# Softmax inverse sums: PE transposes against a VectorE transpose with a round trip through DRAM, and the normalization at another tile

## The chip, the cores and the metric

The kernel runs on one core of a Trainium2 chip. The metric is the device time of one execution in microseconds (us), the median of several. The core's engines run in parallel, each through its own list of instructions in order, and wait for one another through semaphores: TensorE (PE, matmuls; PEld its weight loads), VectorE (DVE), ScalarE (ACT), GpSimd (POOL), and SyncE (SP), which here issues every DMA. The sixteen DMA engines of the core work off what SP issues.

## The reference

Two layers, each added to its input. The first is an attention over 512 tokens with 16 heads of 32, modulated by a conditioning vector; the second rotates quaternions (its filter is the same for all frequencies, so it is a product with a constant matrix). Shapes: x is (8, 512, 512). Cut to what matters:

```python
q, k, v = (proj(Wq), proj(Wk), proj(Wv))                    # H = 16, D = 32
scores = jnp.einsum('bhsd,bhtd->bhst', q, k) * scale
scores = jnp.where(mask[None, None, :, :], -jnp.inf, scores)
attn = jax.nn.softmax(scores, axis=-1)
out = jnp.einsum('bhst,bhtd->bhsd', attn, v)                # -> (B, S, E)
out = out @ Wo.T
rms = jnp.sqrt(jnp.mean(out * out, axis=-1, keepdims=True) + EPS)
xn = out / rms * rms_scale
xn = xn * (1.0 + sc[:, None, :]) + shift[:, None, :]        # sc, shift from the conditioning
x = x + xn
x = x + rotated(x)                                          # Hamilton products with constants
```

The softmax is not normalized in place: the kernel multiplies exp(scores) with v first and scales the result by the inverse of the row sums afterwards.

## The kernel before

**Stages.** `projections` computes q, k and v of all eight batches and leaves them in DRAM (`q_scratch`, `k_scratch`, `v_scratch`). `attention` follows; the change is in it alone.

**Units and tiles.** Attention works in U = 32 units, one for each batch b and group g of four heads (u = 4 b + g). A unit has 16 tiles, one for each head i and block c of 128 query tokens; tile n = 16 u + t is 128 x 512. A tile passes through: `score` on PE (9 tiles ahead), `mask` on DVE (adds the mask, takes the row minimum, into `probs`; some 6 ahead), `exp` on ACT (2 ahead; the row sums go to `den`), `turn` on PE (four 128x128 transposes into one half of `turn_ps`), `move_out` (into `turned_probs`, by DVE for even tiles, ACT for odd). When all 16 tiles of unit u are out, `values(u)` on PE multiplies them with v, at t = 1 of unit u + 1, into `value_ps`: 128 partitions (four heads of 32 dims) by 512 tokens.

**The inverse sums before.** `den` holds a sum per query token on the partitions (128 x 16), but `value_ps` has query tokens along its free axis. So the inverse has to be turned and repeated over the 32 dims of each head: `invert` on DVE at t = 0 (L698), `spread_inverse` on POOL copies it out to 128 x 4 x 128 (L869), `turn_scale` on PE at t = 1, behind `values`, turns that with four transposes into a half of `turn_ps` (L624), `move_scale` on ACT copies it to `inv_T` (L824). `place` counts the halves of `turn_ps`, since the scale takes a 17th place in each unit.

**The norm and what follows.** `norm(u)` on DVE (L713) at t = 3 writes `o_T` = `value_ps` times `inv_T`. POOL's `split` waits for it and cuts o_T into `o_hi` and `o_lo` (L878, L880); POOL then does, in the same iteration and in this order, `rotate` (L518, L911, L913) and `shift` (L888) for a chunk of 128 tokens of the batch before. `project` on PE multiplies o_hi and o_lo with Wo for that batch, one product a tile from t = 2 to 13; `square` (ACT), `rms` (POOL), `rescale` and `residual` (DVE) finish a chunk in the next unit.

**SP's order.** In iteration u SP does: `load_x` for chunk u - 4 (L559), which waits for the rotation of chunk u - 6; `store` of the rotated chunk u - 6 (L563), which waits for the same; `load_unit(u + 2)`, 2 MB of q and k in eight DMAs (L57, L59), which waits until all tiles of unit u are scored (PE gets there at t = 6); where g = 0 `load_mod`, where g = 1 `load_v`. The rotation of chunk u - 6 stands in POOL's iteration u - 1. SP issues in this order and stops at each wait.

**What sets the order.** It is written out by hand: constants (`NORM_AT`, `INVERT_AT`, ...) give the tile at which a step stands, `MASKS` and `EXPS` how many masks and exps DVE and ACT do at each.

Of the kernel before, what the change touches and what calls it, by code (L numbers as in the profile page):

```python
# [8 lines left out]
F32 = mybir.dt.float32  # L9
# [4 lines left out]
P = 128  # L14
# [12 lines left out]
VALUES_AT, SCALE_AT, PROJECT_AT = (1,), 1, 2  # L27
NORM_AT, INVERT_AT, RESCALE_AT, RESIDUAL_AT, SQUARE_AT = 3, 0, 1, 2, 0
# [392 lines left out]
def attention(nc, x, scr, rows, late, qk_stored, mod_scr, out, mask_bias, rot, ident, wo_hi, wo_lo):  # L421
# [3 lines left out]
    with ExitStack() as ctx:  # L425
# [14 lines left out]
        inv = sb("inv", [P, HG, TC])  # L440
        inv_d = sb("inv_d", [P, TC, HG, D])
# [29 lines left out]
        inverted, spread = sem("inverted"), sem("spread")  # L471
        scale_turned, scale_out = sem("scale_turned"), sem("scale_out")
# [14 lines left out]
        def place(n):  # L487

            return n + (n + TILES - SCALE_AT) // TILES - 1

        def scale_place(u):

            return place(min(TILES * (u + 1) + SCALE_AT, N) - 1) + 1

        AT = {place(n): n for n in range(N)}

# [4 lines left out]
        def place_free(eng, at):  # L501

            if at == SCALE_AT - 1:
                at -= 2
            if at in AT and by_act(AT[at]):
                eng.wait_ge(out_act, AT[at] // 2 + 1)
            elif at in AT:
                eng.wait_ge(out_dve, AT[at] // 2 + 1)
            elif at >= SCALE_AT:
                eng.wait_ge(scale_out, (at + 1) // (TILES + 1))  # L510
# [29 lines left out]
        def _(sp):  # L540
# [9 lines left out]

            def load_mod(b):
                if b >= 2:
                    sp.wait_ge(summed, TC * (b - 1))
                sp.dma_start(mod[:, b % 2], mod_scr[b].partition_broadcast(P)).then_inc(mod_in[b % 2], 16)
# [13 lines left out]
            for u in range(U):  # L568
# [29 lines left out]
        def _(pe):  # L598
# [11 lines left out]
            def turn(n):  # L610

                pe.wait_ge(exped, n + 1)
                place_free(pe, place(n) - 2)
                for j in range(TC):
                    last = pe.transpose(turn_ps[:, place(n) % 2, j * P:(j + 1) * P], probs[:, n % RING, j * P:(j + 1) * P],  # L615
                                        ident[:, :])
# [390 lines left out]
```

## Time and profile before

| | us |
|---|---|
| median of 3 runs (lowest, highest) | 912.03 (911.07, 912.26) |
| the profiled execution, its own time | 911.68 |
| its span in the profile | 909.9 |
| PE busy in the span | 854.2 |
| DVE, ACT, POOL busy | 641.4, 613.3, 488.1 |

The attention stage begins near 283 us, and its first inverse is at 303 us; the last tile is turned at about 866 us. Behind that is a tail of some 40 us for the last chunks. The profile lists, for each engine, when it is busy and what ended the idle time before an instruction; "landing" of a DMA is the time from its issue to its semaphore.

### The profile page before, as it was taken

The numbers are of one execution on the slowest core, as the hardware profiler recorded it, in microseconds if no ns is written. First come the engines' busy times: TensorE is split into PE (matmuls) and PEld (weight loads), VectorE is DVE, ScalarE is ACT, GpSimd is POOL, SyncE is SP. The second block draws the span as 40 slices with busy tenths as digits, with TensorE's granted clock in tenths as the row PEclk, the third lists the DMA queues.
The fourth block names the chain that finished last, engine by engine and source line by source line (L and its number), as shares of the span: only waits on it lengthen the run. The fifth ranks groups of instructions, "written<-read, shape, count | busy, mean of one in ns | idle before, by whom it ended". The sixth has DMA issues, their size and how long they took to land.

```text
span 909.9 us, 16967 instructions
## 1 busy us (share of the span) xinstructions
PE 854.2 (94%) x5254; PEld 633.0 (70%) x5254; DVE 641.4 (70%) x1514; ACT 613.3 (67%) x1491; POOL 488.1 (54%) x348
## 2 busy tenths in 40 slices
PE   6999999999995999999999999999999999999970
PEld 5788888888883655776677667766776677667740
DVE  4621321322216887999899989998999899989868
ACT  5222232322215989899989998999899989998920
POOL 0999980000000111377577757775777577757774
PEclk9999999999997999999999999999999999999995
DMA  8844654553497784587667775777578568765201
GB/s 279 327 165 177 226 195 164 217 196 143 181 197 244 167 181 105 140 204 161 159 173 159 162 201 128 161 180 184 128 180 207 137 146 209 159 160 117 70 24 46
DMA packets 82305, 153.74 MB, mean 169 GB/s; under 512 B 8472, under 2 KB 9112, under 8 KB 82224
## 3 DMA queue, kind: packets, MB, share of 16 engines
q1 hardware_dynamic: 82224, 152.75, 62.4%
q8 instruction: 39, 0.64, 0.3%
q14 instruction: 42, 0.34, 0.1%
HBM read 102.35 MB, written 50.36 MB: 168 GB/s over the span
## 4 chain that ended last, share of the span: by engine, by line
PE 58%; DVE 7%; issue 3%; DVEq 0%; ACT 0%; POOL 0%; ACTq 0%
PE turn_ps L615 23%; PE value_ps L641 13%; PE score_ps L607 12%; PE y_ps L657 8%; DVE probs L690 3%; PE turn_ps L624 2%; DVE turned_probs L705 1%; PE score_ps L657 1%; DVE probs L518 1%; DVE probs L764 0%; DVE v_sb L776 0%; DVE least L690 0%; DVE o_T L713 0%; DVEq L514 0%; DVE probs L767 0%
## 5 line engine op out<-in xcount | busy, mean ns | idle before, releaser
L807 ACT ACTIVATE probs<-probs,least 128x512 f32<-128x512 f32 x512 | 363.5, 713 | 4.2 <-DVE least L690 4.1
L690 DVE CUSTOM_DVE_ANT_0 probs<-score_ps,mask_bias 128x512 f32<-128x512 f32 x512 | 331.5, 681 | 38.7 <-PE score_ps L607 36.0
L615 PE MATMUL turn_ps<-ident,probs 128*128 128x128 f32 x2048 | 309.3, 273 | 9.9 <-DVE turned_probs L705 3.9
L615 PEld LDWEIGHTS turn_ps<-ident,probs 128*128 128x128 f32 x2048 | 245.4, 141 | 86.3 <-issue 30.2
L607 PE MATMUL score_ps<-k_rows,q_rows 128*128 128x512 f32 x512 | 247.3, 485 | 9.7 <-PEq L68 9.4
L705 DVE COPY turned_probs<-turn_ps 128x512 f32<-128x512 f32 x256 | 175.9, 687 | 16.2 <-PE turn_ps L615 16.2
L816 ACT ACTIVATE turned_probs<-turn_ps 128x512 f32<-128x512 f32 x256 | 150.9, 590 | 51.2 <-PE turn_ps L615 50.5
L261 DVE SCALAR_TENSOR_TENSOR late<-proj,late 128x512 fp32r<-128x512 f32 x64 | 43.9, 690 | 182.2 <-ACT late L230 182.2
L230 ACT ACTIVATE late<-proj 128x512 fp32r<-128x512 f32 x64 | 38.3, 598 | 128.2 <-PE proj L319 113.2
L518 POOL TENSOR_TENSOR late<-rot,late 128x2048 f32<-128x2048 f32 x27 | 124.3, 4605 | 0.0
L641 PE MATMUL value_ps<-turned_probs,v_sb 128*32 128x512 f32 x1024 | 116.5, 595 | 0.7 <-ACT turned_probs L816 0.7
L878 POOL CAST o_hi<-o_T 128x512 fp32r<-128x512 f32 x32 | 21.4, 670 | 165.4 <-DVE o_T L713 134.5
L607 PEld LDWEIGHTS score_ps<-k_rows,q_rows 128*128 128x128 f32 x512 | 97.8, 191 | 14.0 <-issue 9.8
L807 ACT ACTIVATION_READ_ACCUMULATOR probs<-probs,least 128x1 f32 x512 | 97.7, 191 | 0.0
L915 POOL MEMSET minus_half<- 128x1 f32 x1 | 0.1, 98 | 150.4 <-POOLq L68 150.4
L641 PEld LDWEIGHTS value_ps<-turned_probs,v_sb 128*32 128x32 f32 x1024 | 30.0, 109 | 63.6 <-issue 62.6
L911 POOL TENSOR_TENSOR late<-late 128x1024 f32<-128x1024 f32 x27 | 64.6, 2392 | 2.1
L222 ACT ACTIVATE v_out<-proj 128x512 f32<-128x512 f32 x32 | 18.9, 597 | 62.8 <-PE proj L319 62.8
L317 PE MATMUL proj<-w_hi_v,x_hi 128*128 128x512 f32 x128 | 51.5, 402 | 7.2 <-DVE x_lo L270 7.2
L318 PE MATMUL proj<-w_lo_v,x_hi 128*128 128x512 f32 x128 | 50.9, 398 | 0.0
L319 PE MATMUL proj<-w_hi_v,x_lo 128*128 128x512 f32 x128 | 50.8, 397 | 0.0
L869 POOL COPY inv_d<-inv 128x512 f32<-128x512 f32 x32 | 19.6, 613 | 56.4 <-DVE inv L698 56.4
(112 smaller groups left out, 1289.3 us busy)
## 6 DMA issues: line engine op xcount, KB each, us to landing
q_rows<-q_scratch SPq DMA_DIRECT2D x128, 256.0 KB, 6.0
k_rows<-k_scratch SPq DMA_DIRECT2D x128, 256.0 KB, 6.9
q_scratch<-late SPq DMA_DIRECT2D x64, 256.0 KB, 2.3
k_scratch<-late SPq DMA_DIRECT2D x64, 256.0 KB, 2.3
v_scratch<-v_out SPq DMA_DIRECT2D x32, 256.0 KB, 2.0
v_sb<-v_scratch SPq DMA_DIRECT2D x8, 1024.0 KB, 12.0
raw<-in_xT SPq DMA_DIRECT2D x7, 1024.0 KB, 5.7
late<-in_x SPq DMA_DIRECT2D x28, 256.0 KB, 6.0
```

The costliest lines, as they stand in the source:

```text
L317: pe.matmul(out, hi(k), other_hi(k), start=(k == 0), stop=False)
L318: pe.matmul(out, hi(k), other_lo(k), start=False, stop=False)
L518: return eng.tensor_tensor(to.rearrange("p j (i d) -> p j i d", i=4), rot[:, :, :, :], chunk.rearrange("p (j d) -> p j d", j=4).unsqueeze( ...
L607: pe.matmul(score_ps[:, n % 4, :], rows.q[:, u % 2, i, c * P:(c + 1) * P], rows.k[:, u % 2, i, :], start=True, stop=True).then_inc(scored, 1)
L615: last = pe.transpose(turn_ps[:, place(n) % 2, j * P:(j + 1) * P], probs[:, n % RING, j * P:(j + 1) * P], ident[:, :])
L641: last = pe.matmul(value_ps[i * D:(i + 1) * D, :], v_sb[:, b % 2, j, h * D:(h + 1) * D], turned_probs[:, (HG * u + i) % SLOTS, j, :], star ...
L657: last = pe.matmul(y, left[:, b % 2, k, t], right[:, k, :], start=(part == 0), stop=(part == 11))
L690: dve.tensor_tensor_reduce(probs[:, n % RING, :], score_ps[:, n % 4, :], mask_bias[:, c, :], 1.0, 3e38, ALU.add, ALU.min, least[:, n // TI ...
L705: dve.tensor_copy(turned_probs[:, h % SLOTS, :, n % TC * P:(n % TC + 1) * P], turn_ps[:, place(n) % 2, :].rearrange("p (j t) -> p j t", j= ...
L807: act.activation(probs[:, n % RING, :], probs[:, n % RING, :], ACT.Exp, bias=least[:, u % 2, n % TILES:n % TILES + 1], scale=-1.0, accum_o ...
L816: act.activation(turned_probs[:, h % SLOTS, :, n % TC * P:(n % TC + 1) * P], turn_ps[:, place(n) % 2, :].rearrange("p (j t) -> p j t", j=T ...
L911: pool.tensor_tensor(mix[:, 0:2, :], mix[:, 0:2, :], mix[:, 2:4, :], ALU.add).then_inc(paired, 1)
```

## The change

The inverse no longer passes through POOL, PE and ACT. DVE writes the reciprocals into the first 16 columns of a 128 x 32 tile (the rest is set to zero once), and turns that by its transpose of 32 x 32 blocks into `inv_turn`: each of the four blocks of 32 partitions then has the 16 sums as rows and 32 query tokens as columns. SP writes the four blocks into a DRAM tensor of 16 x 128 (`inv_scratch`), waits until they have landed, and reads from it for each of the four heads one row of 512 elements into 32 partitions of `inv_T`. The norm waits for these four loads, and stands at t = 6 instead of 3. `turn_scale`, `move_scale`, POOL's `spread_inverse` and the 17th place of `turn_ps` are gone; tile n now uses half n % 2, and its `turn` waits for the copy of tile n - 2.

```diff
-VALUES_AT, SCALE_AT, PROJECT_AT = (1,), 1, 2
-NORM_AT, INVERT_AT, RESCALE_AT, RESIDUAL_AT, SQUARE_AT = 3, 0, 1, 2, 0
+VALUES_AT, PROJECT_AT = (1,), 2
+NORM_AT, INVERT_AT, RESCALE_AT, RESIDUAL_AT, SQUARE_AT = 6, 0, 1, 2, 0
...
-        inv = sb("inv", [P, HG, TC])
-        inv_d = sb("inv_d", [P, TC, HG, D])
+        inv = sb("inv", [P, 32])
+        inv_turn = sb("inv_turn", [P, 32])
...
+        def moved_out(eng, n):
+
+            if n >= 0:
+                eng.wait_ge(out_act if by_act(n) else out_dve, n // 2 + 1)
...
+            def spread_inverse(u):
+                sp.wait_ge(inv_turned, u + 1)
+                if u > 0:
+                    for i in range(HG):
+                        sp.wait_ge(inv_in[i], 16 * u)
+                for a in range(TC):
+                    sp.dma_start(scr["inv"][:, a * D:(a + 1) * D],
+                                 inv_turn[a * D:a * D + TILES, :]).then_inc(inv_stored, 16)
+                sp.wait_ge(inv_stored, 64 * (u + 1))
+                if u > 0:
+                    sp.wait_ge(normed, u)
+                for i in range(HG):
+                    sp.dma_start(inv_T[i * D:(i + 1) * D, :],
+                                 scr["inv"][i * TC:(i + 1) * TC, :].rearrange("c q -> (c q)").partition_broadcast(D)
+                                 ).then_inc(inv_in[i], 16)
...
                 if u >= NG + 2:
                     store((u - NG - 2) // NG, (u - NG - 2) % NG)
+                if u > 0:
+                    spread_inverse(u - 1)
                 if u + 2 < U:
                     load_unit(u + 2)
...
+            spread_inverse(U - 1)
             sp.wait_ge(valued, NG * (B - 1))
...
                 pe.wait_ge(exped, n + 1)
-                place_free(pe, place(n) - 2)
+                moved_out(pe, n - 2)
...
-            def turn_scale(u):
-
-                pe.wait_ge(spread, u + 1)
-                place_free(pe, scale_place(u) - 2)
-                for c in range(TC):
-                    last = pe.transpose(turn_ps[:, scale_place(u) % 2, c * P:(c + 1) * P],
-                                        inv_d[:, c].rearrange("p i d -> p (i d)"), ident[:, :])
-                last.then_inc(scale_turned, 1)
...
                 if u > 0:
-                    dve.wait_ge(spread, u)
-                dve.reciprocal(inv[:, :, :], den[:, u % 2]).then_inc(inverted, 1)
+                    dve.wait_ge(inv_turned, u)
+                dve.reciprocal(inv[:, 0:TILES].rearrange("p (i c) -> p i c", i=HG), den[:, u % 2]).then_inc(inverted, 1)
+                dve.wait_ge(inverted, u + 1)
+                if u > 0:
+                    dve.wait_ge(inv_stored, 64 * u)
+                dve.transpose(inv_turn[:, :], inv[:, :]).then_inc(inv_turned, 1)
...
                 dve.wait_ge(valued, u + 1)
-                dve.wait_ge(scale_out, u + 1)
+                for i in range(HG):
+                    dve.wait_ge(inv_in[i], 16 * (u + 1))
...
-            def move_scale(u):
-                act.wait_ge(scale_turned, u + 1)
-                if u > 0:
-                    act.wait_ge(normed, u)
-                act.activation(inv_T[:, :], turn_ps[:, scale_place(u) % 2, :], ACT.Copy).then_inc(scale_out, 1)
...
-            def spread_inverse(u):
-                pool.wait_ge(inverted, u + 1)
-                if u > 0:
-                    pool.wait_ge(scale_turned, u)
-                pool.tensor_copy(inv_d[:, :, :, :], inv[:, :, :].rearrange("p i c -> p c i").unsqueeze(3)
-                                 .to_broadcast([P, TC, HG, D])).then_inc(spread, 1)
...
+    scr["inv"] = nc.dram_tensor("inv_scratch", (TILES, P), F32, kind="Internal").ap()
```

SP's list in the middle of attention, at the end of an iteration with g = 0 and the start of the next, before (`late<-in_x` is load_x, `out<-late` the store):

```order
L554 DMA mod_b<-mod_scratch 128x1024 [waits summed]
L559 DMA late<-in_x 128x512 [waits rotated]
L563 DMA out<-late 128x512 [waits rotated]
L57 DMA q_rows<-q_scratch 32x4x512 [waits scored]
L59 DMA k_rows<-k_scratch 32x4x512
```

and after:

```order
L555 DMA mod_b<-mod_scratch 128x1024 [waits summed]
L560 DMA late<-in_x 128x512 [waits rotated]
L564 DMA out<-late 128x512 [waits rotated]
L542 DMA inv_scratch<-inv_turn 16x32 [waits inv_in2,inv_in1,inv_in3,inv_in0,inv_turned]
L542 DMA inv_scratch<-inv_turn 16x32 x3
L548 DMA inv_T<-inv_scratch 32x512 [waits normed,inv_stored]
L548 DMA inv_T<-inv_scratch 32x512 x3
L57 DMA q_rows<-q_scratch 32x4x512 [waits scored]
```

The eight DMAs of the inverse, with two waits, now stand between the store and the loads of q and k.

DVE's list around the old place of the norm (t = 2 and 3 of a unit), before; the rows L690 are the masks, L705 the copies of turned tiles, L729 the residual:

```order
L729 SCALAR_TENSOR_TENSOR late<-scaled,rstd,late 128x512 [waits shifted,rstd_ready,scaled_ready]
L690 ISA probs,least<-score_ps,mask_bias 128x512 [waits scored,turned]
L690 ISA least 128x1
L713 TENSOR_TENSOR o_T<-value_ps,inv_T 128x512 [waits o_ready,scale_out,valued]
L705 COPY turned_probs<-turn_ps 128x4x128 [waits valued,turned]
```

and from there to its new place (t = 5 to 7), after, where the masks are L682 and the copies L701:

```order
L701 COPY turned_probs<-turn_ps 128x4x128 [waits valued,turned]
L682 ISA probs,least<-score_ps,mask_bias 128x512 [waits scored,turned]
L682 ISA least 128x1
L710 TENSOR_TENSOR o_T<-value_ps,inv_T 128x512 [waits inv_in2,inv_in3,inv_in1,o_ready,inv_in0,valued]
L682 ISA probs,least<-score_ps,mask_bias 128x512 [waits scored,turned]
L682 ISA least 128x1
L701 COPY turned_probs<-turn_ps 128x4x128 [waits valued,turned]
```

The norm has moved from ahead of the copy of tile 2 to ahead of a mask and the copy of tile 6, and waits for the four loads instead of ACT's copy.

## Rows read from the trace of the kernel before

**Rows 1.** Page, parts 1 and 4: busy us (share) xinstructions; chain by engine.

```profile
PE 854.2 (94%) x5254; PEld 633.0 (70%) x5254; DVE 641.4 (70%) x1514; ACT 613.3 (67%) x1491; POOL 488.1 (54%) x348
...
PE 58%; DVE 7%; issue 3%; DVEq 0%; ACT 0%; POOL 0%; ACTq 0%
```

**Rows 2.** Windows: busy us of PE, PEld, DVE, ACT, POOL (instructions), clock, DMA, GB/s.

```profile
400.00:500.00 100.00, 99.32 (x701) 72.43 (x700) 92.28 (x244) 91.22 (x237) 72.10 (x49) 1.00 0.69 160
```

**Rows 3.** Timeline, DVE: start, duration, line, tiles; norms (L713) and reciprocals (L698).

```profile
381.46 0.69 DVE L713 TENSOR_TENSOR o_T<-value_ps,inv_T 128x512 f32<-128x512 f32 x1
...
575.34 0.24 DVE L698 RECIPROCAL inv<-den 128x16 f32<-128x16 f32 x1
...
581.42 0.69 DVE L713 TENSOR_TENSOR o_T<-value_ps,inv_T 128x512 f32<-128x512 f32 x1
...
854.59 0.69 DVE L713 TENSOR_TENSOR o_T<-value_ps,inv_T 128x512 f32<-128x512 f32 x1
...
865.59 0.24 DVE L698 RECIPROCAL inv<-den 128x16 f32<-128x16 f32 x1
871.22 0.69 DVE L713 TENSOR_TENSOR o_T<-value_ps,inv_T 128x512 f32<-128x512 f32 x1 [1.89 <-ACT inv_T L824]
```

**Rows 4.** Chain in order of time: start, us; the four transposes of one unit.

```profile
852.93 0.59 PE turn_ps L624 x4
```

**Rows 5.** Timeline, DVE and PE, around the copy of tile 6.

```profile
585.09 0.68 DVE L690 CUSTOM_DVE_ANT_0 probs<-score_ps,mask_bias 128x512 f32<-128x512 f32 x1
...
585.70 0.68 DVE L705 COPY turned_probs<-turn_ps 128x512 f32<-128x512 f32 x1
...
586.86 0.60 PE L615 MATMUL turn_ps<-ident,probs 128*128 128x128 f32 x4
```

**Rows 6.** SP's waits (us in total, times, longest); timeline of POOL, subtraction and rotation.

```profile
SPq L559 <- POOL late L913: 108.8, 26, 17.4
...
582.97 1.30 POOL L880 TENSOR_TENSOR o_lo<-o_T,o_hi 128x512 fp32r<-128x512 f32 x1
...
591.37 1.29 POOL L913 TENSOR_TENSOR late<-late 128x512 f32<-128x512 f32 x1
```

**Rows 7.** Timeline, SP: start of each DMA issue, its us, line, tiles.

```profile
585.01 0.33 SPq L57 DMA_DIRECT2D q_rows<-q_scratch  x1
...
592.68 0.35 SPq L559 DMA_DIRECT2D late<-in_x  x1
593.07 0.44 SPq L563 DMA_DIRECT2D out<-late  x1
603.22 0.33 SPq L57 DMA_DIRECT2D q_rows<-q_scratch  x1
603.59 0.43 SPq L59 DMA_DIRECT2D k_rows<-k_scratch  x1
604.07 0.43 SPq L57 DMA_DIRECT2D q_rows<-q_scratch  x1
...
611.25 0.90 SPq L563 DMA_DIRECT2D out<-late  x1
```

**Rows 8.** DMA us to landing, issued 865.81, 847.64, 593.07, 611.25; then two busy windows.

```profile
out<-late SPq DMA_DIRECT2D x1, 256.0 KB, 2.0
...
late<-in_x SPq DMA_DIRECT2D x1, 256.0 KB, 2.7
...
out<-late SPq DMA_DIRECT2D x1, 256.0 KB, 7.4
...
out<-late SPq DMA_DIRECT2D x1, 256.0 KB, 9.4
...
588.00:590.00 2.00, 2.00 (x17) 1.73 (x15) 2.00 (x7) 2.00 (x6) 1.92 (x2) 1.00 1.05 205
...
616.00:618.00 2.00, 2.00 (x17) 1.51 (x14) 1.02 (x4) 2.00 (x6) 0.00 (x0) 1.00 1.04 383
```

**Rows 9.** Chain in order of time: PE's last products.

```profile
870.50 9.11 PE score_ps L657 x39
```

More of the change, by code:

```diff
@@ L470, in attention @@
         out_act, out_dve = sem("out_act"), sem("out_dve")
-        inverted, spread = sem("inverted"), sem("spread")
-        scale_turned, scale_out = sem("scale_turned"), sem("scale_out")
+        inv_set, inverted, inv_turned = sem("inv_set"), sem("inverted"), sem("inv_turned")
+        inv_stored = sem("inv_stored")
+        inv_in = [sem(f"inv_in{i}") for i in range(HG)]
         valued, normed = sem("valued"), sem("normed")
@@ L485, in attention @@
         rotated = sem("rotated")
[L487 to L495, printed above, removed]
         def by_act(n):
             return n % 2 == 1
[L501 to L510, printed above, removed]
+        def moved_out(eng, n):
+            if n >= 0:
+                eng.wait_ge(out_act if by_act(n) else out_dve, n // 2 + 1)
         def take_waits(eng):
@@ L612, in turn @@
                 pe.wait_ge(exped, n + 1)
-                place_free(pe, place(n) - 2)
+                moved_out(pe, n - 2)
                 for j in range(TC):
-                    last = pe.transpose(turn_ps[:, place(n) % 2, j * P:(j + 1) * P], probs[:, n % RING, j * P:(j + 1) * P],
+                    last = pe.transpose(turn_ps[:, n % 2, j * P:(j + 1) * P], probs[:, n % RING, j * P:(j + 1) * P],
                                         ident[:, :])
                 last.then_inc(turned, 1)
-            def turn_scale(u):
-                pe.wait_ge(spread, u + 1)
-                place_free(pe, scale_place(u) - 2)
-                for c in range(TC):
-                    last = pe.transpose(turn_ps[:, scale_place(u) % 2, c * P:(c + 1) * P],
-                                        inv_d[:, c].rearrange("p i d -> p (i d)"), ident[:, :])
-                last.then_inc(scale_turned, 1)
             def values(u, part):
@@ L666, in _ @@
                     values(u - 1, VALUES_AT.index(t))
-                if t == SCALE_AT and u > 0:
-                    turn_scale(u - 1)
                 if n + SCORE_AHEAD < N:
@@ L675, in _ @@
                 values(U - 1, part)
-            turn_scale(U - 1)
             for parts in (range(9), range(9, 12)):
@@ L705, in move_out @@
                 dve.tensor_copy(turned_probs[:, h % SLOTS, :, n % TC * P:(n % TC + 1) * P],
-                                turn_ps[:, place(n) % 2, :].rearrange("p (j t) -> p j t", j=TC)).then_inc(out_dve, 1)
+                                turn_ps[:, n % 2, :].rearrange("p (j t) -> p j t", j=TC)).then_inc(out_dve, 1)
             def norm(u):
                 dve.wait_ge(valued, u + 1)
-                dve.wait_ge(scale_out, u + 1)
+                for i in range(HG):
+                    dve.wait_ge(inv_in[i], 16 * (u + 1))
                 if u > 0:
@@ L730, in residual @@
                                          ALU.mult, ALU.add).then_inc(summed, 1)
-            done = 0
+            dve.memset(inv[:, :], 0.0).then_inc(inv_set, 1)
+            dve.wait_ge(inv_set, 1)
             for n in range(MASK_AHEAD):
@@ L816, in move_out @@
                 act.activation(turned_probs[:, h % SLOTS, :, n % TC * P:(n % TC + 1) * P],
-                               turn_ps[:, place(n) % 2, :].rearrange("p (j t) -> p j t", j=TC),
+                               turn_ps[:, n % 2, :].rearrange("p (j t) -> p j t", j=TC),
                                ACT.Copy).then_inc(out_act, 1)
-            def move_scale(u):
-                act.wait_ge(scale_turned, u + 1)
-                if u > 0:
-                    act.wait_ge(normed, u)
-                act.activation(inv_T[:, :], turn_ps[:, scale_place(u) % 2, :], ACT.Copy).then_inc(scale_out, 1)
             def square(m):
@@ L846, in _ @@
                     square(u - NG - 1)
-                if t == SCALE_AT and u > 0:
-                    move_scale(u - 1)
                 if by_act(n - 1) and n > 0:
@@ L852, in _ @@
             square(CHUNKS - 1)
-            move_scale(U - 1)
             for c in range(TC):
@@ L917, in _ @@
             for u in range(U):
-                if u > 0:
-                    spread_inverse(u - 1)
                 if u > NG:
@@ L927, in _ @@
                     shift(u - NG)
-            spread_inverse(U - 1)
             rms(CHUNKS - 1)
```

## The prediction

> **What bounds the kernel now.** I read first the page's busy shares and chain, then the busy time by windows, because the share over the whole span mixes the projection stage with the attention stage that the change edits. TensorE is busy 94% of the span, and of the chain that ended last 58% is PE [rows 1]. In the attention stage it is plainer: from 400 to 500 us PE is busy 99.3 of 100 us, while DVE and ACT stand at 92 and 91 [rows 2]. So a microsecond of PE work is worth a microsecond there, and DVE and ACT have about 8% to spare. The repeating piece is a unit (16 tiles). From the norm (L713) of unit 5 to that of unit 31 there are 26 intervals: 854.59 - 381.46 = 473.1 us, or **18.20 us a unit** [rows 3]. An edit that touches every unit is judged against this number.
>
> **What is removed.** Each of the 32 units loses four PE transposes (L624), the ACT copy (L824) and the POOL copy (L869). The four transposes take 0.59 us of the chain [rows 4], and as PE is the bound they are worth that: the floor of a unit falls to 18.20 - 0.59 = **17.6 us**. ACT's and POOL's part lies off the path and is worth nothing by itself. The slot that the scale took in the two-deep turn_ps ring goes too; I give it nothing, since PE hardly waits.
>
> **What is added on DVE.** One 32x32 transpose of 128x32, with a wait for the reciprocal before it. The trace has no such transpose; the nearest rows are the reciprocal of 128x16 (0.24 us) [rows 3] and a 128x512 copy (0.68 us) [rows 5], so it costs 0.1 to 0.7 us a unit, and I take 0.3, near the small one. DVE has some 1.4 us a unit free (8% of 18.2), so the path sees nothing of it; the masks queued behind it have no late customer either, because PE is then in the value matmuls. If that cover were gone, 0.3 us a unit would come on top, 10 us in all. The memset ahead of the loop is one instruction, in a stretch where DVE waits for scores.
>
> **What is moved: the norm, and what hangs on it.** The norm goes from t=3 to t=6. Behind it on DVE are a mask and the copy of tile 6, and PE's turn of tile 8 waits for that copy. In the unit shown that turn starts at 586.86, and the copy takes 0.68 us [rows 5]; with norm and mask ahead of it at 0.61 us each (585.70 less 585.09, the pitch at which DVE starts such operations), the norm must start by 586.86 - 0.68 - 0.61 - 0.61, about 584.9. That is 3.5 us after its old place (581.42), 9.5 us after the reciprocal (575.34) [rows 3], and 8.9 us after it once PE's 0.59 us are gone. Taken from the reciprocal alone, the new route fits. That is not where it starts, though.
>
> **The queue that the route is put into.** SP runs in order, and the eight new DMAs are written behind load_x and store of the same iteration. Both wait for POOL's rotation of the iteration before; SP waits there 26 times, 108.8 us in all [rows 6]. That rotation stands on POOL behind split, which waits for the norm. So the norm of one unit now gates the inverse of the next unit, and that gates the next norm: **a loop once round per unit that did not exist before**. If it is longer than 17.6 us, its length sets the time.
>
> Step by step. From the norm's start (581.42 [rows 3]) through POOL's cast, subtraction and rotation, whose last step ends at 591.37 + 1.29 = 592.66 [rows 6], to SP's load_x at 592.68 [rows 7] it is **11.26 us**. The POOL copy that is removed stood ahead of split's wait, so nothing of this shrinks. From load_x to store 0.39 us, and DMAs behind one another start every 0.47 us (603.59, 604.07) [rows 7]: the first store of the inverse starts 0.86 us after load_x, the fourth 1.41 later. It lands after L1; the next four start over another 1.41 us, and the last lands after L2. With 0.05 us for SP to wake, a loop is 11.26 + 0.86 + 1.41 + L1 + 0.05 + 1.41 + L2 = **15.0 + L1 + L2**.
>
> L1 and L2 are not in the trace: stores of 16x32 elements, and loads of 64 KB that read one row for 32 partitions. The nearest rows are 256 KB transfers on an empty queue: a store lands in 2.0 us, a load in 2.7 [rows 8]. These are the upper ends. For the lower ends I take the moving of 256 KB out of them, 0.7 us at 383 GB/s for the store and 1.3 us at 205 for the load, the fast and the slow rate at which busy windows run [rows 8]; that leaves 1.3 and 1.4. I choose 1.8 and 2.2, nearer the upper ends, because four transfers of small pieces have no reason to land at the very floor. Then a loop is **19.0 us**, 1.4 over the floor (bounds 17.7 and 19.7).
>
> The Trainium skill (DMA: Bandwidth & Descriptors, section "Anatomy of one DMA — SWDGE (gpsimd) path") gives a DMA about 2.0 us of fixed cost, mostly the receipt of the write and heaviest at HBM, plus its bytes at 436 GB/s. That speaks against two hops through DRAM; by it L1 would be an estimated 2.0 and L2 2.15, the loop 19.15, and the sum some 3 us higher. For a 256 KB store it would give 2.6 us where the row shows 2.0, so the trace's own rows are used.
>
> **Queueing.** All of it shares one queue. From the first q load of a unit to the landing of its store, a unit with the modulation load takes 593.07 + 7.4 - 585.01 = 15.5 us, one with the v load 611.25 + 9.4 - 603.22 = 17.4 [rows 7, 8]; a plain unit is shorter. In the loop the q loads come 1 to 1.6 us before the norm (behind the inverse loads, when PE has scored the sixth tile while DVE still waits), and the 256 KB of inverse loads, 1.2 us, are added. So the store lands 15.5 + 1.2 - 1 = 15.7 or 17.4 + 1.2 - 1.6 = 17.0 us after the norm, and the inverse stores 0.2 behind it. By themselves they would land at 11.26 + 0.86 + 1.41 + 1.8 = 15.3. So the modulation unit is held up by 0.6, the v unit by 1.9, the plain one not: loops of 19.0, 19.6 and 20.9 us. Of the 26 loops 14 are plain and 6 each of the others: (14 x 19.0 + 6 x 19.6 + 6 x 20.9) / 26 = **19.6 us**, 1.4 over the 18.20 of now, or 26 x 1.4 = +36 us.
>
> **Before and behind the loops.** Units 1 to 5 have no rotation in the loop; each gains its 0.59 us, as does the tail: 6 x 0.59 = -3.5 us. In the tail the inverse lands 0.5 + 1.41 + 1.8 + 0.05 + 1.41 + 2.2 = 7.4 us after the last reciprocal (865.59), at 873.0 where the norm now is at 871.22 [rows 3]. PE first runs 36 of its 48 last products, which need nothing of it: until about 870.50 - 0.59 + 36/48 x 9.11 = 876.7 [rows 9]. From a norm's start to the end of the subtraction it is 582.97 + 1.30 - 581.42 = 2.9 us [rows 3, 6], so that ends at 875.9 and just fits. If that cover is gone, at most the 1.8 us of delay are lost.
>
> **Sum.** 909.9 + 36 - 3.5 = 942 us of span; the profiled execution took 911.68, 1.8 more than its span, and the median is 0.35 above it: **944 us**, 3.5% slower.
>
> **The rivals.**
> (a) *The loop does not bind, and the kernel is faster.* One mechanism: both hops land so fast that the loop stays under 17.6 us, that is L1 + L2 under 2.6 us with no queueing. Then each of 32 units keeps its 0.59 us: 912 - 19 = 893. For it: SP's wait and POOL's idle time are harmless today, and from the reciprocal alone there would be 8.9 us. Against it: the lower ends that I could find sum to 2.7, and the modulation and v units still queue. 8%.
> (b) *About the same* (910 to 914): L1 + L2 near 3.2 and hardly any queueing. 4%.
> (c) *The queue decides in every unit*: small writes, or reads of one row, land late, or the 2 MB of q and k hold up all units as I have it for the v units. All loops of 21 us: 909.9 + 26 x 2.8 - 3.5 + 2.2 = 981. 13%.
> (d) The forecast: slower by the loop, 918 to 972 us. 75%. With L1 + L2 at 2.7 the plain loops would be near 18.1, but the queue would end last in the others (15.5 + 1.2 + 0.2 + 2.9 = 19.8, and 20.1): 19.0 on average and 929 us. With 2.0 and 2.7, 19.7 plain and 20.1 on average, 957 us; 0.5 us more on each hop gives another 15 to 26 us.
>
> The range of 915 to 975 leaves out (a), (b) and most of (c). Changes below 0.2% (1.8 us) can hardly be told from none; faster by more has 8%, within it 4%, slower 88%.
>
> **What would show it.** Right: the norm's interval from unit 6 on is 18.5 to 21 us instead of 18.20, with a period of four units; DVE idles 1 to 3 us ahead of the norm, released by a load of inv_T; PE waits ahead of the turn of tile 8; SP's first inverse store starts 0.9 us after load_x, not after the transpose; from norm to load_x it is still 11.26 us. The first units should be shorter than now. Wrong: SP waiting at the inverse store for DVE's transpose rather than at load_x for POOL, no idle time ahead of the norm, or two hops that together land in under 2.7 us.

## The result and the profile after

Line numbers of the changed kernel: reciprocal L690, DVE's transpose L694, norm L710, residual L726; SP's stores of the inverse L542, its loads L548, load_x L560, store L564; PE's turn L619, score L611, tail products L652; POOL's split L860 and L862, rotation L503, L893, L895, rms L881.

| | before | after |
|---|---|---|
| median us (lowest to highest) | 911.81 (4 runs) | 952.01 (949.39 to 953.22, 4 runs) |
| ratio | | 1.0438 (1.0414 to 1.0462) |
| span of the profiled execution | 909.9 | 947.5 |
| norm of iteration 5 to that of iteration 31 | 473.1 | 508.27 |
| a unit (26 of them) | 18.20 | 19.55 |

The profiled execution of the changed kernel took 949.39 us, the shortest of its four. One of the four runs of e8 below, 947.24 us, was in a slow state of the chip; the ratio there leaves it out, the median does not.

The page of the changed kernel, busy time and the chain by engine, against [rows 1]:

```profile
PE 846.5 (89%) x5126; PEld 620.1 (65%) x5126; DVE 655.6 (69%) x1547; ACT 602.8 (64%) x1459; POOL 468.7 (49%) x316
...
POOL 28%; DMA 10%; issue 10%; SPq 9%; DVE 7%; PE 5%; DVEq 0%; POOLq 0%
```

PE's share of the chain that ended last fell from 58% to 5%; POOL, the DMAs and SP's queue took its place. The stretch of [rows 2] again:

```profile
400.00:500.00 100.00, 88.39 (x619) 61.71 (x618) 85.63 (x226) 81.39 (x211) 60.50 (x40) 1.00 0.69 162
```

PE is no longer full: 88.4 of 100 us instead of 99.3. One plain unit, DVE's timeline of the changed kernel:

```profile
583.17 0.69 DVE L710 TENSOR_TENSOR o_T<-value_ps,inv_T 128x512 f32<-128x512 f32 x1
...
591.96 0.24 DVE L690 RECIPROCAL inv<-den 128x16 f32<-128x16 f32 x1
592.23 0.21 DVE L694 STREAM_TRANSPOSE inv_turn<-inv 128x32 f32<-128x32 f32 x1
...
602.18 0.69 DVE L710 TENSOR_TENSOR o_T<-value_ps,inv_T 128x512 f32<-128x512 f32 x1 [0.88 <-DMA inv_T<-inv_scratch]
```

and SP's timeline in the same unit:

```profile
594.43 0.35 SPq L560 DMA_DIRECT2D late<-in_x  x1
594.83 0.62 SPq L564 DMA_DIRECT2D out<-late  x1
595.62 1.76 SPq L542 DMA_DIRECT2D inv_scratch<-inv_turn  x4
598.56 1.70 SPq L548 DMA_DIRECT2D inv_T<-inv_scratch  x4
```

The turned inverse is ready at 592.44, but SP's first store of it starts at 595.62, behind load_x at 594.43, which is 11.26 us after the norm of 583.17. That is the loop: 11.26 to load_x, 1.19 to the first store, 2.94 to the first load, 3.62 to the next norm, 19.01 in all. The waits of the whole span, first DVE's and PE's, then SP's:

```profile
PE turn_ps L619 <- DVE turned_probs L701: 44.8, 36, 2.9
...
DVE o_T L710 <- DMA inv_T<-inv_scratch: 37.6, 27, 2.6
```

```profile
SPq L560 <- POOL late L895: 224.8, 26, 13.0
...
SPq L548 <- DMA inv_scratch<-inv_turn: 55.0, 32, 3.8
```

SP's wait at load_x doubled against [rows 6] (224.8 instead of 108.8 us). It is now a wait with customers: the norm stands 27 times for the inverse, and PE's turns stand behind it.

### The profile page after: what moved, and what is told of

Read it like the earlier page. It is cut to its first block, busy times and chain, and to the rows that moved or that the text cites. A ratio compares the mean times of both kernels' runs of the same rounds, so it can differ in the third digit from the quotient of the medians.

```text
span 947.5 us, 17028 instructions
## 1 busy us (share of the span) xinstructions
PE 846.5 (89%) x5126; PEld 620.1 (65%) x5126; DVE 655.6 (69%) x1547; ACT 602.8 (64%) x1459; POOL 468.7 (49%) x316
## 4 chain that ended last, share of the span: by engine, by line
POOL 28%; DMA 10%; issue 10%; SPq 9%; DVE 7%; PE 5%; DVEq 0%; POOLq 0%
POOL late L503 12%; POOL late L893 6%; DMA inv_scratch<-inv_turn 5%; DMA inv_T<-inv_scratch 5%; SPq L542 4%; POOL o_lo L862 4%; POOL late L895 3%; SPq L548 3%; DVE probs L682 2%; PE turn_ps L619 2%; POOL o_hi L860 2%; DVE o_T L710 2%; PE value_ps L636 2%; SPq L564 1%; DVE turned_probs L701 1%
## 5 line engine op out<-in xcount | busy, mean ns | idle before, releaser
L619 PE MATMUL turn_ps<-ident,probs 128*128 128x128 f32 x2048 | 312.4, 275 | 53.5 <-DVE turned_probs L701 44.8
L682 DVE CUSTOM_DVE_ANT_0 probs<-score_ps,mask_bias 128x512 f32<-128x512 f32 x512 | 335.4, 684 | 7.5 <-PE score_ps L611 7.5
L619 PEld LDWEIGHTS turn_ps<-ident,probs 128*128 128x128 f32 x2048 | 243.0, 141 | 134.6 <-issue 54.9
L611 PE MATMUL score_ps<-k_rows,q_rows 128*128 128x512 f32 x512 | 247.2, 486 | 9.2 <-PEq L68 9.1
L701 DVE COPY turned_probs<-turn_ps 128x512 f32<-128x512 f32 x256 | 176.0, 687 | 19.2 <-PE turn_ps L619 19.1
L860 POOL CAST o_hi<-o_T 128x512 fp32r<-128x512 f32 x32 | 21.4, 669 | 275.7 <-DVE o_T L710 234.3
L611 PEld LDWEIGHTS score_ps<-k_rows,q_rows 128*128 128x128 f32 x512 | 98.5, 193 | 39.8 <-DVE least L682 28.1
L503 POOL TENSOR_TENSOR late<-rot,late 128x2048 f32<-128x2048 f32 x27 | 124.2, 4601 | 0.0
L893 POOL TENSOR_TENSOR late<-late 128x1024 f32<-128x1024 f32 x27 | 64.1, 2375 | 2.1
L222 ACT ACTIVATE v_out<-proj 128x512 f32<-128x512 f32 x32 | 18.9, 597 | 62.6 <-PE proj L319 62.6
L317 PE MATMUL proj<-x_hi,w_hi_k 128*128 128x512 f32 x128 | 49.8, 389 | 0.0
```

What stands on the lines that cost most here:

```text
L317: pe.matmul(out, hi(k), other_hi(k), start=(k == 0), stop=False)
L503: return eng.tensor_tensor(to.rearrange("p j (i d) -> p j i d", i=4), rot[:, :, :, :], chunk.rearrange("p (j d) -> p j d", j=4).unsqueeze( ...
L611: pe.matmul(score_ps[:, n % 4, :], rows.q[:, u % 2, i, c * P:(c + 1) * P], rows.k[:, u % 2, i, :], start=True, stop=True).then_inc(scored, 1)
L619: last = pe.transpose(turn_ps[:, n % 2, j * P:(j + 1) * P], probs[:, n % RING, j * P:(j + 1) * P], ident[:, :])
L682: dve.tensor_tensor_reduce(probs[:, n % RING, :], score_ps[:, n % 4, :], mask_bias[:, c, :], 1.0, 3e38, ALU.add, ALU.min, least[:, n // TI ...
L701: dve.tensor_copy(turned_probs[:, h % SLOTS, :, n % TC * P:(n % TC + 1) * P], turn_ps[:, n % 2, :].rearrange("p (j t) -> p j t", j=TC)).th ...
```

## The experiments

All medians are of 4 runs; the kernel before took 911.1 to 911.9 us beside them. "A unit" is the mean over the 26 intervals of the norm from iteration 5 to 31, "plain" the usual interval with no held-up inverse; both are of the profiled execution, which can lie some us beside the median (934.09 against 939.03 us in e1).

| kernel | us | ratio to before | a unit | plain |
|---|---|---|---|---|
| e1_inverse_first | 939.03 | 1.0315 (1.0285 to 1.0344) | 18.95 | 18.05 |
| e2_norm_at_8 | 965.21 | 1.0596 (1.0579 to 1.0614) | 20.17 | 20.2 |
| e4_short_rotation | 940.58 | 1.0302 (1.0263 to 1.0341) | 19.16 | 18.05 |
| e5_before_norm_6 | 923.30 | 1.0135 (1.0118 to 1.0152) | 18.53 | 18.53 |
| e7_loads_early | 944.35 | 1.0334 (1.0292 to 1.0376) | 19.47 | 18.05 |
| e8_shift_first | 936.35 | 1.0230 (1.0210 to 1.0251) | 19.24 | 18.05 |
| e9_residual_4 | 949.87 | 1.0401 (1.0357 to 1.0446) | 19.50 | 18.71 |
| e10_shift_only | 951.32 | 1.0434 (1.0416 to 1.0451) | 19.53 | 19.0 |
| e11_v_on_act | 919.79 | 1.0093 (1.0076 to 1.0110) | 18.34 | 18.05 |
| e12_values_split | 928.01 | 1.0187 (1.0169 to 1.0204) | 18.69 | 18.38 |
| e14_before_split | 918.07 | 1.0069 (1.0052 to 1.0086) | 18.46 | 18.46 |
| e15_norm_at_3 | 894.42 | 0.9810 (0.9794 to 0.9826) | 17.67 | 17.67 |

My theory was the loop through load_x. Against it stood explanations in which POOL's rotation has no part: the inverse's own way from the reciprocal to the norm, or the queue of q, k and v.

**The loop through load_x, cut.** Only SP's list changes:

```diff
+                if u > 0:
+                    spread_inverse(u - 1)
                 if u >= NG:
                     load_x(b - 1, g)
                 if u >= NG + 2:
                     store((u - NG - 2) // NG, (u - NG - 2) % NG)
-                if u > 0:
-                    spread_inverse(u - 1)
```

> One edit to the changed kernel: SP issues the eight DMAs of the inverse ahead of load_x and store in each iteration, so that they no longer stand behind POOL's rotation; nothing else. Theory A (the loop norm, split, rotation, load_x, inverse, norm sets 19.55 us a unit): the loop is cut. The inverse then starts 0.5 us after the reciprocal; in plain units it lands some 7 us after it where 8.9 are allowed, so the unit falls to the floor of PE near 17.6; units with the modulation or the v load ahead in the queue stall by some 0.6 and 2.8 us. Average about 18.4, span 915 to 922, ratio to before 1.00 to 1.01. SP's wait at load_x for POOL disappears or shrinks to under 30 us in all. Theory B (the round trip through DRAM is too long for tile 6 wherever it starts): 940 to 952, ratio 1.03 to 1.045. Theory C (contention of the DMAs with q and k): no great change either, above 940.

13 us came back, less than expected: 939 us lies just under what theories B and C had, so the median doesn't decide between them and A. The single units do. SP's waits of e1 no longer list load_x; it waits for DVE's transpose instead:

```profile
SPq L542 <- DVE inv_turn L694: 187.6, 32, 10.1
...
SPq L548 <- DMA inv_scratch<-inv_turn: 87.4, 32, 6.6
```

Plain units fell from 19.01 to 18.05, with no wait at the norm: the loop was real, and worth 0.96 a unit. But 18.05 is not my floor of 17.6, and something else took up to 3 us in some units. The next runs are about both.

**The same loop, shortened on POOL.** The middle addition of the rotation works on 64 columns instead of 1024:

```diff
-                pool.tensor_tensor(mix[:, 0:2, :], mix[:, 0:2, :], mix[:, 2:4, :], ALU.add).then_inc(paired, 1)
+                pool.tensor_tensor(mix[:, 0:1, 0:64], mix[:, 0:1, 0:64], mix[:, 2:3, 0:64], ALU.add).then_inc(paired, 1)
```

> Left out: of POOL's middle addition in the rotation of a chunk (128x1024, 2.4 us) all but 64 columns, so the rotated chunks of the main part are not the reference's; all waits stay. The loop becomes some 2.2 us shorter from norm to load_x (11.26 to about 9.1 us). Theory A: the unit falls by 0.7 to 1.9 us, to 17.7 to 18.8 (the queue behind q and k, or PE's floor, then ends last), so 900 to 930, though POOL is idle for more than 6 us of each unit in the changed kernel. Theories B and C (length of the round trip alone, contention of DMAs): POOL is half idle and off the path, no change, 945 to 955.

The addition fell from 2.37 to 0.32 us and the kernel by 11 us, although POOL is busy for half of the span only. The time, 940.58 us, is outside theory A's 900 to 930 and outside the 945 to 955 of B and C. What it shows is that the length of POOL's rotation counts: explanations without POOL in the path fall. The shortest units again end at 18.05, so 17.0 for the loop (19.0 - 2.05) was not reached: the same second bound.

**The norm later still.**

```diff
-NORM_AT, INVERT_AT, RESCALE_AT, RESIDUAL_AT, SQUARE_AT = 6, 0, 1, 2, 0
+NORM_AT, INVERT_AT, RESCALE_AT, RESIDUAL_AT, SQUARE_AT = 8, 0, 1, 2, 0
```

> One number in the changed kernel: the norm stands at tile 8 instead of 6, 1.8 us later on PE. Theory A (loop): the deadline moves, but so does the start, since load_x follows the norm by a fixed 11.26 us; the unit stays at 19.5 us, ratio to before 1.035 to 1.05. Theory B (the round trip is measured from the reciprocal and misses tile 6 by 1.0 to 2.3 us): the stalls of plain units go to zero and those of v units to 0.5, 26 x 1.3 = 34 us less, about 915, ratio 1.00 to 1.01.

Slower than either expectation. The norm never waits for a DMA; DVE waits for POOL (e2, timeline of DVE):

```profile
588.64 0.68 DVE L710 TENSOR_TENSOR o_T<-value_ps,inv_T 128x512 f32<-128x512 f32 x1
...
602.08 0.75 DVE L726 SCALAR_TENSOR_TENSOR late<-scaled,rstd,late 128x512 f32<-128x512 f32 x1 [2.90 <-POOL rstd L881]
...
608.82 0.69 DVE L710 TENSOR_TENSOR o_T<-value_ps,inv_T 128x512 f32<-128x512 f32 x1
```

A second loop: norm, split, rotation, shift, rms on POOL, residual on DVE 13.44 us later, and 6.74 us to the next norm, 20.18. At t = 6 the same sum is 13.49 + 4.55 = 18.04 in e1 (norm 441.23, residual 454.72, norm 459.27). That fits the 18.05 so well that I took it for the second bound (theory L2). It was wrong, as the next runs show.

**The norm's place alone.** The kernel before with `NORM_AT` 6 instead of 3, everything else as it was.

> The kernel before with one number changed: the norm at tile 6 instead of 3, the inverse still through POOL, PE and ACT. Theory A: the norm's place alone costs nothing, since nothing there closes the loop (the inverse does not wait for POOL's rotation through SP): 910 to 914, ratio 0.998 to 1.003, with SP's wait at load_x some 2.7 us longer in each unit. A rival by which the later norm itself costs the time (POOL's work, the products of the batch before, or the next unit's residual come late): up to 26 x 1.35 = 35 us more, 930 to 950.

12 us slower, where I had expected nothing. The first units have no rotation, no rescale and no residual yet, and they are as long as the others (e5, DVE's timeline):

```profile
330.98 0.68 DVE L713 TENSOR_TENSOR o_T<-value_ps,inv_T 128x512 f32<-128x512 f32 x1
...
349.49 0.69 DVE L713 TENSOR_TENSOR o_T<-value_ps,inv_T 128x512 f32<-128x512 f32 x1
```

18.51, where the kernel before has 17.93 there: 0.58, nearly the 0.61 at which DVE starts such operations. It speaks for a theory without POOL (D): at t = 3 DVE stands anyway, because PE is in the value products and delivers no scores; at t = 6 it has no free time, and the norm pushes the masks and copies on which PE's turns wait. PE's waits for DVE's copies in two of these units, in e5 (321.23 to 358.27) and then in the kernel before (320.95 to 356.81), bear it out:

```profile
PE turn_ps L615 <- DVE turned_probs L705: 2.9, 6, 0.9
```

```profile
PE turn_ps L615 <- DVE turned_probs L705: 1.7, 6, 0.3
```

That is 0.6 us more in each unit, the whole difference. In the later units the place costs less, 0.33 (18.53 against 18.20).

**L2 against D.** Three kernels share a base, e7, in which SP has the inverse first and the modulation and v loads ahead of `load_unit`. e8 adds `shift` ahead of `split` on POOL, e9 instead puts the residual at t = 4 (`RESIDUAL_AT` 4). e10 has e8's order on POOL, but SP's list of the changed kernel.

> The changed kernel with SyncE's list put in another order: the inverse's DMAs first in a unit (as in e1_inverse_first), and the modulation and v loads ahead of the next rows' load instead of behind it. Theory V (what e1 still lost behind a v load is the queue: the 1 MB is issued late in a unit, just ahead of the next unit's inverse, the norm then waits 1.7 to 3.0 us, TensorE stands over 2 us and runs at a lower granted clock afterwards): the waits behind v loads and the slow stretches after them go, all units take the 18.05 us of e1's plain ones; e1 had 18.95 on average over 26 intervals, so its span of 932.2 falls by about 23 to 909, some 911 us in all, ratio 1.00. Theory W (the low clock has another cause than the wait, or the load's bytes disturb whatever place they have): units behind a v load stay near 20, 930 us or more.

> e7_loads_early with GpSimd's list in another order as well: the addition of the shift to the next block of x ahead of the split of o instead of behind the rotation. Theory L2 (e1's 18.05 us of a unit are a second loop: norm, split, rotation, shift 1.3, rms and rstd on GpSimd, residual, norm): that loop gets 1.3 shorter, another bound ends it at 17.6 to 17.8, and 26 intervals give 6 to 11 us: 900 to 905 us, ratio 0.988 to 0.994. Theory D (the 18.05 are the round of VectorE and TensorE over one unit, in which the norm at the seventh tile stands among VectorE's work instead of in its wait for TensorE): shift's place does nothing, the same time as e7.

> e7_loads_early with VectorE's residual at the fifth tile of a unit instead of the third. Theory L2 (the second loop through GpSimd sets 18.05): the residual no longer waits for rstd, and the loop gets about 2 us of slack: units of 17.6 to 17.8, as in e8. Theory D (round of VectorE and TensorE): the residual leaves VectorE's wait for TensorE in the third tile and stands in a stretch where VectorE has no free time, so a unit gets longer by up to its 0.67 us: 18.4 to 18.7, 920 to 928 us, slower than e7.

> The changed kernel as it is, SyncE's list untouched, with GpSimd's shift ahead of the split alone. Theory L1 (in the changed kernel the loop norm, split, rotation, x load, store, inverse DMAs, norm binds at 19.0 in plain units; shift is not in it): the norm still waits for the inverse's DMA in nearly every unit, plain units stay at 19.0, 947 to 955 us. Theory L2 (the second loop binds here too): 1.0 to 1.3 less in a unit, 915 to 925 us.

L2 falls twice. With the shift out of its way (e8) plain units stay at 18.04; with two tiles of slack for the residual (e9) they get longer, 18.71. Timeline of DVE in e9:

```profile
598.51 0.75 DVE L726 SCALAR_TENSOR_TENSOR late<-scaled,rstd,late 128x512 f32<-128x512 f32 x1
601.00 0.69 DVE L710 TENSOR_TENSOR o_T<-value_ps,inv_T 128x512 f32<-128x512 f32 x1
...
619.70 0.69 DVE L710 TENSOR_TENSOR o_T<-value_ps,inv_T 128x512 f32<-128x512 f32 x1
```

The residual waits for nothing there, and costs 0.66 a unit merely by standing later on DVE, as D says. The medians are no test here, because the waits of e7 behind v loads (below) stay in e8 and e9 too: e9 took 949.87 us against D's 920 to 928, and e8's runs (931 to 947) overlap those of e7 (937 to 946). e10 confirms the loop through load_x in the changed kernel: shift is not in it, and nothing moved (19.0 plain, 951.32 against 952.01).

e7 itself missed. Its plain units are e1's, but behind five of the six v loads the norm waits 3.4 to 6.4 us (1.7 to 3.0 in e1). SP's timeline of e7 behind a v load, and the landing of these stores:

```profile
464.86 1.71 SPq L542 DMA_DIRECT2D inv_scratch<-inv_turn  x4
474.79 1.70 SPq L548 DMA_DIRECT2D inv_T<-inv_scratch  x4
```

```profile
inv_scratch<-inv_turn SPq DMA_DIRECT2D x4, 2.0 KB, 6.9
```

Four stores of 2 KB took 9.9 us from the first issue to the loads. x, out, v, q and k, 3.5 MB, had been issued on the same queue 5 to 12 us earlier, and I put it down to them. Another place in that queue doesn't help.

**The v load on ScalarE's queue.** e1, with the v load issued by ACT at t = 2 of the unit, ahead of SP's q and k loads (queue and place change together here; which of them did it isn't separated):

```diff
-                if g == 1 and b + 1 < B:
-                    load_v(b + 1)
...
+                if t == 2 and u % NG == 1 and u // NG + 1 < B:
+                    load_v(u // NG + 1)
```

> e1_inverse_first with the v load (1 MB once in four units) issued by ScalarE at the third tile of its unit, so on another DMA queue and in the stretch in which the queue of SyncE stands empty, instead of by SyncE behind the next rows' load. Theory Q (what e1, and more so e7, lost in the unit behind a v load: the inverse's four small stores stand in the same queue behind 3.5 MB instead of 2.5 MB, and the engines take some 200 GB/s while the rotation runs): the norm's waits behind v loads fall from 1.7 to 3.0 us to under 0.7, the low clock behind them goes too, all units come near 18.05, and of e1's 23 us of excess over 26 units some 18 to 23 go: a span of 909 to 914, 911 to 916 us, ratio 1.00 to 1.005. Theory W (1 MB more in the unit disturbs whatever queue and place it has): the waits stay over 1.5 us, 930 to 940 us.

Most of what Q says: 19 us less than e1, though 4 more than its range. No unit behind a v load waits any more; what is left is 1.2 to 1.7 us in the v unit itself, whose inverse loads now run beside it (iteration 29 has a modulation load ahead of it as they have, but no v load, and its norm doesn't wait):

```profile
461.86 0.69 DVE L708 TENSOR_TENSOR o_T<-value_ps,inv_T 128x512 f32<-128x512 f32 x1 [1.72 <-DMA inv_T<-inv_scratch]
```

**The value products in two pieces.** e11, and the kernel before, with `VALUES_AT = (1, 2)`.

> e11_v_on_act with the 32 value products of a unit put at two tiles in TensorE's list (16 at the second, 16 at the third) instead of all at the second. Theory D (the 18.05 us of e7, e8 and e11 are a round of VectorE and TensorE: VectorE stands still while TensorE runs 3.6 us of value products, and the norm at the seventh tile no longer fills that stand): with half the block each time VectorE stands less, and a unit comes to 17.5 to 17.8, 6 to 14 us less than e11: 900 to 908 us, ratio 0.987 to 0.997. Against it (the round is set by TensorE's own work): 18.05 as before, the time of e11.

> The kernel before with its value products at two tiles in the same way (16 at the second, 16 at the third). Theory D: in the kernel before the norm at the fourth tile fills VectorE's stand, so there is little to gain: 17.95 to 18.2 a unit, 904 to 911 us. If TensorE's block of value products costs the kernel before as much as the changed one, 17.6 a unit and 894 us, and the changed kernel has no edge even in its best form.

Both got slower, by 0.33 and 0.26 a unit; TensorE's 32 products take 3.64 us in one piece and 1.92 + 1.92 in two. So DVE's stand behind the block can't be had this way, and D in the form "half the block, half the stand" is wrong.

**The norm back at its old place, with all else new.** It multiplies by a tile that stands in SBUF, so it need not wait for the inverse:

```diff
-                for i in range(HG):
-                    dve.wait_ge(inv_in[i], 16 * (u + 1))
...
-                dve.tensor_tensor(o_T[:, :], value_ps[:, :], inv_T[:, :], ALU.mult)
+                dve.tensor_tensor(o_T[:, :], value_ps[:, :], f32(wo_hi[:, 0, :]), ALU.mult)
```

> e11_v_on_act with the norm back at the fourth tile of a unit, as in the kernel before. So that it has no DMA to wait for, it multiplies by a tile of weights that stands in SBUF all the time; the inverse is still made, turned, stored and loaded as in e11, but nothing uses it (so the output is not the reference's). What is measured is the worth of the norm's place with all the added and removed instructions in it. Theory D (of the 18.05 us of e11 some 0.3 to 0.45 come from the norm at the seventh tile, where VectorE has no free time and TensorE's transposes wait for VectorE's copies; my floor of 17.6, TensorE's 18.20 less its four transposes, holds for the norm at its old place): units of 17.6 to 17.75, and no wait of the norm behind modulation loads (seven of 1.2 to 1.7 us in e11): a span of 896 to 903, 898 to 905 us, ratio 0.985 to 0.993. Theory T (the four transposes were worth only 0.15 of a unit in time, the place nothing): 18.0 to 18.05 a unit, 907 to 910 us.

The product is then not the attention's output. 17.67 in every unit, 0.38 below e11's plain ones: D's size of the norm's place. What DVE's place does to PE shows in the waits of PE's weight loads for the turns, in three plain units of e11 (470.63 to 524.77) and then of e15 (460.77 to 513.77):

```profile
PEld turn_ps L617 <- issue: 3.6, 9, 0.6
...
PEld turn_ps L617 <- ACT probs L803: 0.7, 3, 0.2
```

```profile
PEld turn_ps L617 <- issue: 1.3, 3, 0.4
```

In these units of e15 none waits for ACT's exps. "Issue" names no releaser, so how the place comes to its 0.38 us is shown only in part.

Theory T falls (it named 18.0 and more). The time is even below D's range: of the 26.0 us of span between e11 and e15, 19.1 lie between the reciprocals of iterations 5 and 31, 4.5 ahead of them and 2.3 behind.

Of the variants of the changed kernel whose norm uses the inverse, none beats the kernel before; the nearest is e11, 0.9% slower. A version with both the early norm and the route through DRAM would need the inverse at t = 3, and no run has one.

## Why the prediction came out

The forecast was 944 us, the time is 952, inside the range. The direction, the mechanism and the length of the loop were right. The floor under the loop was wrong, which the time does not show, because the loop's own length decides. In the queueing two errors in opposite directions hid one another, and that is luck. The 8 us that are missing are not in the loops (35.1 us instead of 36) but at the two ends (+2.5 instead of -3.5) and in the median, which lies 2.6 us over the profiled execution where the forecast had 0.35.

**The parts of a unit**, as the runs give them, against the prediction's:

| step | predicted | measured | by |
|---|---|---|---|
| four transposes and their copies gone, less what is added | -0.59 | -0.53 | 18.20 to 17.67, e15 |
| the norm at t = 6 | 0 | +0.38 | 17.67 to 18.05, e11 |
| the loop through load_x, plain | +1.4 | +0.96 | 18.05 to 19.01, e1 and after |
| queueing, mean of 26 | +0.6 | +0.54 | 19.01 to 19.55 |
| sum | +1.4 | +1.35 | |

**What is removed**: right. PE is the bound of the kernel before, and 0.59 of chain was worth 0.53, with DVE's transpose (0.21 us where I took 0.3) and the new DMAs already in it; no run took these apart.

**The failed step: the floor of 17.6 us, with nothing for the move of the norm itself.** That the route fits, taken from the reciprocal alone, was right: in e1's plain units the norm doesn't wait. But I asked only whether the norm would be late for the copy of tile 6. I did not ask what DVE did at t = 3 and at t = 6. In the kernel before, DVE stands just ahead of the norm's old place, for a score that PE delivers only behind the value products: 2.24 us in an early unit and 0.98 in a later one (timeline of DVE, kernel before):

```profile
326.43 0.69 DVE L690 CUSTOM_DVE_ANT_0 probs<-score_ps,mask_bias 128x512 f32<-128x512 f32 x1 [2.24 <-PE score_ps L607]
...
580.81 0.69 DVE L690 CUSTOM_DVE_ANT_0 probs<-score_ps,mask_bias 128x512 f32<-128x512 f32 x1 [0.98 <-PE score_ps L607]
```

The norm follows these masks at 327.04 and 581.42, and e5 and e15 show that it costs less there. My argument that DVE has 8% to spare used a mean over the unit, and the slack is not spread evenly: of the 1.5 us of the later unit 0.98 are this one stand. So the floor was 18.05, not 17.6, and the loop's 19.0 stood 0.96 above it instead of 1.4. As the loop's own length decides, the time did not show this error; had the loop not bound, rival (a) would have been some 12 us too fast (an estimate: 32 x 0.38).

**The loop**: right, term by term. Norm to load_x 11.26 (predicted 11.26), to the first store 1.19 (0.86), to the first load 2.94 (1.41 + 1.8 + 0.05 = 3.26), to the norm 3.62 (1.41 + 2.2 = 3.61): 19.01 against 19.0. Without the 1.41 us of issue, L1 is about 1.5 and L2 2.2. The Trainium skill (DMA: Bandwidth & Descriptors, "Anatomy of one DMA — SWDGE (gpsimd) path") states a fixed cost of about 2.0 us for DMAs that GpSimd issues. These are SP's, and the 64 KB loads, at 2.0 median from issue to landing, agree; the stores of the plain unit come out shorter.

```profile
inv_T<-inv_scratch SPq DMA_DIRECT2D x128, 64.0 KB, 2.0
```

**Queueing**: the sum is right, the split is not. Units behind a v load took 20.1 on average (predicted 20.9; five 19.9 to 20.8, one 19.11), behind a modulation load 19.4 (predicted 19.6; five 18.9 to 19.5, one 20.65), all others 19.4 (predicted 19.0). What the prediction did not have makes up the difference: the two units after the first v unit took 20.38 and 19.55, single inverse loads landed in 3.5 to 3.6 us instead of 2.0 (iterations 31 and 9, units of 20.28 and 20.65), and there are stretches of a low TensorE clock (below; 19.75 and 19.63). Why the first two came about stays open. In rival (d) the modulation loop of 19.8 leaves out the 1 us that the forecast takes off; with it, it is 18.8, and that case comes to some 922 us.

**Before and behind the loops**: wrong by 6 us (+2.5 instead of -3.5). The five first units were to gain 3.0 us, but the reciprocal of iteration 5 came 0.65 us later than before (375.68 against 375.02): the norm's place costs in them too (17.81 a unit at first, where the kernel before has 17.93 and e15 17.50), and the first norm stood 1.26 us for its inverse. The tail was to gain 0.6; from the last reciprocal to the end it took 46.11 us instead of 44.28. Its norm came 8.63 us after that reciprocal (predicted 7.4), and its cover was costed with a steady-state row: 2.9 us from the norm's start to the end of the subtraction. In the tail of the changed kernel it is 5.6 us:

```profile
910.04 0.69 DVE L710 TENSOR_TENSOR o_T<-value_ps,inv_T 128x512 f32<-128x512 f32 x1 [2.34 <-DMA inv_T<-inv_scratch]
...
910.65 2.28 DVE L503 TENSOR_TENSOR probs<-rot,late 128x2048 f32<-128x2048 f32 x1
...
910.90 2.50 POOL L860 CAST o_hi<-o_T 128x512 fp32r<-128x512 f32 x1 [4.04 <-DVE o_T L710]
...
913.48 2.12 POOL L862 TENSOR_TENSOR o_lo<-o_T,o_hi 128x512 fp32r<-128x512 f32 x1
...
915.65 0.51 PE L652 MATMUL score_ps<-wo_hi,o_hi 128*128 128x512 f32 x1 [1.56 <-POOL o_lo L862]
```

The cast takes 2.50 instead of 0.61 us beside DVE's 128x2048 product, the subtraction 2.12 instead of 1.28, and PE's last products wait 1.56. The row for this was in the trace of the kernel before, whose tail has the same slow cast:

```profile
872.08 2.50 POOL L878 CAST o_hi<-o_T 128x512 fp32r<-128x512 f32 x1 [3.59 <-DVE o_T L713]
```

With the 5.6 us, the subtraction of the forecast would have ended at 878.6, past PE's cover (876.7). 35.1 us in the loops and 2.5 at the ends make 37.6 us, the difference of the spans; the forecast had +36 and -3.5.

**The signs named**: most were seen. The norm's intervals are 18.9 to 20.8, DVE stands ahead of the norm for 1.4 us on average (37.6 / 27), PE stands ahead of the turn, the first store follows load_x (1.19 us behind it instead of 0.9). The period of four units is blurred by what the queueing did not have. The first units are hardly shorter than before, which was the one sign against me, and it pointed at the norm's place.

## What to carry to other kernels

A step that is put behind another engine's wait in an in-order queue makes a loop if that wait hangs on the step's own result one round earlier; add its length up before asking whether the step fits. A step that is moved costs what its new place is worth: look at what its engine did at either place, not at its mean share. And a small DMA whose landing somebody waits for is better not queued behind megabytes that nobody waits for yet: moving the 1 MB load of v, one in four units, to another queue and an earlier place was worth 19 us here.

## What the hardware showed

**The clock after a stall.** After some of the norm's waits PE ran at its lower level for several us. In e1, around 558 us (the columns are those of [rows 2]):

```profile
556.00:558.00 2.00, 0.00 (x0) 0.00 (x0) 1.21 (x2) 0.49 (x2) 0.35 (x1) 0.90 0.79 263
558.00:560.00 2.00, 1.16 (x5) 1.19 (x6) 1.95 (x8) 0.81 (x2) 1.92 (x3) 0.50 0.93 258
560.00:562.00 2.00, 2.00 (x8) 1.60 (x8) 1.87 (x5) 0.33 (x1) 2.00 (x1) 0.50 1.07 223
562.00:564.00 2.00, 2.00 (x9) 1.50 (x8) 0.62 (x2) 1.67 (x5) 2.00 (x1) 0.50 1.06 218
564.00:566.00 2.00, 2.00 (x13) 1.74 (x12) 0.92 (x4) 1.16 (x3) 1.92 (x2) 0.89 1.07 212
```

PE had stood for 3.21 us. At the granted clock of 0.50, which is the level of 1.2 GHz, it ran 8 or 9 instructions in 2 us ([rows 8] have 17 at 1.00), 13 in the window in which the clock rose, and the next reciprocal came 11.39 us after the norm instead of 8.78: 2.6 us on top of the 2.98 of the wait. In the changed kernel the same cost 1.6 us behind the norms of iterations 14 and 26, after stands of 2.15 and 2.01 us. Not each stall has it: after 2.87 us of standing in iteration 6 of the changed kernel the next reciprocal came after 8.79. What decides wasn't tried.

**POOL beside DVE.** The 2.50 us of the cast in the tail, against 0.61 elsewhere, start 0.25 us after DVE's product of two SBUF tiles of 2.28 us, and end 0.47 us after its end. The tail of the kernel before has the same pair, 0.25 us apart and 2.50 us long. The Trainium skill (SBUF — State Buffer, "SBUF: two separate sides") has such a pair of instructions exclude one another for a whole instruction; these rows agree. No run here took the product away.
